# The cross-attention's mask written into the score banks by ScalarE and VectorE, with the order of the steps made anew

## The chip, the core and the metric

The kernel runs on one core of a Trainium2 chip. Its five engines run side by side and meet only at semaphores: TensorE (PE, with the load of its stationary operand shown apart as PEld), VectorE (DVE), ScalarE (ACT), GpSimd (POOL) and SyncE (SP), which issues most DMAs. The time is device time of one execution in microseconds (us). Three runs of the kernel before took 546.56, 554.24 and 556.15 us, a median of 554.24. The execution that the profile shows took 546.79 us.

## The reference, cut to what matters

One decoder layer on 16 sequences of 100 tokens, 256 wide: self-attention (16 heads of 16, rotary), cross-attention (16 heads of 64), and a feed-forward layer that sends every token to one of 14 experts, each with a residual and a layer norm. What the change touches is the mask of the cross-attention:

```python
scores = einsum('bhsk,bhtk->bhst', Q, K) / sqrt(64)
causal_ok = arange(Sk)[None, :] <= arange(Sq)[:, None]
pad_ok = arange(Sk)[None, :] < source_seq_len[:, None]
allowed = causal_ok[None, None] & pad_ok[:, None, None, :]
attn = softmax(where(allowed, scores, -1e6), axis=-1)
```

The mask depends on the sequence and not on the head. The context has 361 tokens, and the causal rule leaves the first 100 of them.

## The kernel before, in words

The attention part is one list of 1819 steps, `STEPS`, written out by hand or by a program. Every engine walks through the same list and does the steps that are its own; a step that needs another engine's result waits on a semaphore. So the list alone sets the order in which an engine takes its work, and an engine that waits holds back all that stands behind it in its own queue. After the list comes the experts' part, a loop over blocks of 128 rows.

Names of steps are `kind.side.sequence.half.unit`: side `s` is self-attention, `x` is cross-attention. A sequence has two halves of its heads, a half is a *pair* of units, a unit has 4 heads and a score tile of 100 x 400. The steps of one pair of the cross-attention:

- `scores` (TensorE): at L1298 two matmuls add the mask, `ident_neg` (the unit matrix times -1e6) times `mask_b`, one for each unit's bank, and open the banks; then at L1303 eight matmuls per unit's four heads and two units add the products of queries and keys. The two units use the upper and lower 64 rows of the array.
- `max` (VectorE, L1030), `exp` (ScalarE, L886, four instructions for the heads of a unit, each with its sum), `inv` (VectorE, L1035), `norm` (GpSimd, L798), `turn` (TensorE transposes, L1314), `copy_v` or `copy_a` (VectorE L1042 or ScalarE L895, out of the one bank for turned tiles), `pv` (TensorE, L1340), `o_hi` (ScalarE, L907) and `o_lo` (VectorE, L1050), then `wo`, `added`, `stats`, `rstd`, `ln` and the router.

Four banks hold scores: pairs take two of them in turn, so that the scores of pair p wait for the `exp` of pair p-2. The self-attention's `scores` fill all four. The projections `xT`, `qk`, `K`, `V`, `Q`, `wo` and others share two further banks. The weights `W_self`, `W_K`, `W_V`, `W_O` are split at the start into a high part (`w_hi`, ScalarE) and a low part (`w_lo_v` on VectorE at L961, `w_lo_p` on GpSimd at L773). `keys_v` (VectorE, L1024) or `keys_p` (GpSimd, L791) spreads the self-attention's keys.

Of the kernel before, what the change touches and what calls it, by code (L numbers as in the profile page):

```python
# [82 lines left out]
qkT_out.1 turn.s.0.0.0 mask.0 exp.s.0.1.1 K.0.1 keys_p.1 copy_v.s.0.0.0 rot_sum.2 w_hi.9 turn.s.0.0.1 inv.s.0.1
mask.1 norm.s.0.1.0 scores.s.1.0 copy_v.s.0.0.1 K_out.0.1 w_lo_v.9 norm.s.0.1.1 turn.s.0.1.0 K_out.0.0 pv.s.0.0
w_hi.10 max.s.1.0.0 qkT.2 qk.3 copy_v.s.0.1.0 qkT_out.2 w_lo_p.10 max.s.1.0.1 o_hi.s.0.0 exp.s.1.0.0 max.s.1.1.0
turn.s.0.1.1 o_lo.s.0.0 keys_v.2 K.0.2 copy_v.s.0.1.1 exp.s.1.0.1 max.s.1.1.1 qk_out.3 pv.s.0.1 exp.s.1.1.0
inv.s.1.0 v.2 rot.3 norm.s.1.0.0 o_hi.s.0.1 norm.s.1.0.1 exp.s.1.1.1 turn.s.1.0.0 o_lo.s.0.1 copy_v.s.1.0.0 v_out.2
turn.s.1.0.1 K_out.0.2 inv.s.1.1 out.0 rot_sum.3 norm.s.1.1.0 copy_a.s.1.0.1 scores.s.2.0 added.s.0 norm.s.1.1.1
stats.s.0 pv.s.1.0 turn.s.1.1.0 o_hi.s.1.0 max.s.2.0.0 rstd.s.0 qkT.3 copy_a.s.1.1.0 o_lo.s.1.0 V.0.0 max.s.2.0.1
qkT_out.3 ln.s.0 exp.s.2.0.0 keys_p.3 max.s.2.1.0 x_load.4 turn.s.1.1.1 V_out.0.0 yT.0 exp.s.2.0.1 bias.x.0  # L90
copy_v.s.1.1.1 K.0.3 yT_out_v.0 max.s.2.1.1 exp.s.2.1.0 inv.s.2.0 pv.s.1.1 norm.s.2.0.0 V.0.1 o_hi.s.1.1
norm.s.2.0.1 exp.s.2.1.1 o_lo.s.1.1 turn.s.2.0.0 V_out.0.1 K_out.0.3 copy_v.s.2.0.0 v.3 inv.s.2.1 norm.s.2.1.0
# [1596 lines left out]
```

How the kernel before makes its waits and increments, by code:

```python
    def __call__(self, sem, value):  # L310
        if self.seen.get(id(sem), 0) < value:
            self.seen[id(sem)] = value
            self.engine.wait_ge(sem, value)
# [417 lines left out]
                def check(b):  # L731
                    wait(lens_in, 16)
                    length = pool.value_load(len_row[0:1, b:b + 1])
                    with pool.If(length <= 0):
                        step, dma = fix_step, fix_dma[b]
                        pool.memset(fix_b[:, :], 0.0).then_inc(step, 1)
                        pool.wait_ge(step, 5 * b + 1)
                        pool.dma_start(fix_a[:, :], ctx[b, 0:P, :]).then_inc(dma, 16)
                        pool.dma_start(fix_b[0:TK - 2 * P, :], ctx[b, 2 * P:TK, :]).then_inc(dma, 16)
                        pool.wait_ge(dma, 32)
                        pool.tensor_tensor(fix_b[:, :], fix_a[:, :], fix_b[:, :], ALU.add).then_inc(step, 1)
                        pool.wait_ge(step, 5 * b + 2)
                        pool.dma_start(fix_a[:, :], ctx[b, P:2 * P, :]).then_inc(dma, 16)
                        pool.wait_ge(dma, 48)
                        pool.tensor_tensor(fix_b[:, :], fix_a[:, :], fix_b[:, :], ALU.add).then_inc(step, 1)
                        pool.wait_ge(step, 5 * b + 3)
                        pool.partition_all_reduce(fix_a[:, :], fix_b[:, :], P, bass.bass_isa.ReduceOp.add).then_inc(step, 1)
                        pool.wait_ge(step, 5 * b + 4)
# [844 lines left out]
    @block.vector  # L1593
# [13 lines left out]
        dve.wait_ge(tables_in, 32)
        dve.wait_ge(counts_ready, 1)
```

## Time and profile before

| | |
|---|---|
| time of the profiled execution | 546.79 us |
| its span, first to last instruction | 545.0 us |
| median of three runs | 554.24 us |
| TensorE busy | 486.0 us, 89% |
| VectorE busy | 361.8 us, 66% |
| ScalarE busy | 322.8 us, 59% |
| GpSimd busy | 216.1 us, 40% |
| mean granted clock of TensorE | 0.967 |

The page shows one execution. Section 1 gives each engine's busy time, section 2 cuts the span into 40 slices, and section 5 lists groups of instructions with their busy time, the mean length of one, and the idle time of the engine before them with what ended it. Busy shares are averages over stages: the attention's list takes the span up to about 456 us, the experts the rest from 465 us. A matmul's record is longer than its share of the engine, because matmuls overlap; the distance from one start to the next is what it takes.

### The profile page before, as it was taken

How to read it: one execution, taken by the hardware profiler on the slowest of the kernel's cores; microseconds unless marked ns; L12 is line 12 of the kernel's file. 1: busy time of each engine (PE TensorE's matmuls, PEld its weight loads, DVE VectorE, ACT ScalarE, POOL GpSimd, SP SyncE). 2: the span in 40 equal slices, each digit the busy share in tenths (PEclk: the TensorE clock that was granted, in tenths of full speed). 3: DMA queues.
4: the chain of work that ended last, by engine and by line, in shares of the span. 5: the costliest groups of instructions: out<-in, count | busy, mean ns of one | idle time of the engine just before them, and what ended most of it. 6: DMA issues, size and time to landing. Idle time of an engine off the chain costs nothing. (4 is left out here: it accounts for less than half of the span.)

```text
span 545.0 us, 13058 instructions
## 1 busy us (share of the span) xinstructions
PE 486.0 (89%) x4614; PEld 414.3 (76%) x4614; DVE 361.8 (66%) x1007; ACT 322.8 (59%) x1481; POOL 216.1 (40%) x309
## 2 busy tenths in 40 slices
PE   0667999999899999999999999999999871999992
PEld 0456787888689879888987888798798670899991
DVE  1788678688955875888588668856653833355563
ACT  2366678875747586867386876757573821433430
POOL 2246444443622553345245523543340511044343
PEclk9868999999999999999999999999999996899998
DMA  8960002910045008004500440180404522999300
GB/s 206 201 126 2 9 16 113 292 67 1 25 155 162 14 12 304 6 9 169 171 1 25 154 157 1 58 274 4 138 35 155 169 81 73 335 371 370 112 26 16
DMA packets 37577, 62.85 MB, mean 115 GB/s; under 512 B 9979, under 2 KB 30721, under 8 KB 36793
## 3 DMA queue, kind: packets, MB, share of 16 engines
q1 hardware_dynamic: 34668, 57.86, 32.8%
q0 software_dynamic: 1888, 3.30, 1.9%
q10 hardware_dynamic: 950, 0.80, 0.6%
q8 instruction: 39, 0.64, 0.5%
q14 instruction: 32, 0.26, 0.1%
HBM read 58.65 MB, written 29.77 MB: 162 GB/s over the span
## 5 line engine op out<-in xcount | busy, mean ns | idle before, releaser
L886 ACT ACTIVATE probs<-bank,neg_max 100x100 f32<-100x100 f32 x512 | 170.5, 379 | 17.9 <-DVE neg_max L1030 13.5
L798 POOL TENSOR_TENSOR probs<-probs,row_inv 100x400 f32<-100x400 f32 x128 | 112.1, 896 | 128.6 <-DVE row_inv L1035 128.6
L886 ACT ACTIVATION_READ_ACCUMULATOR probs<-bank,neg_max 100x1 f32 x512 | 123.3, 241 | 0.0
L1314 PE MATMUL bank<-ident,probs 100*100 100x100 f32 x512 | 67.3, 254 | 5.9 <-DVE probsT L1042 5.0
L1030 DVE TENSOR_REDUCE neg_max<-bank 100x4 f32<-100x400 f32 x128 | 68.2, 563 | 6.2 <-PE bank L1303 4.6
L1314 PEld LDWEIGHTS bank<-ident,probs 100*100 100x100 f32 x512 | 49.4, 128 | 18.3 <-issue 8.0
L1042 DVE COPY probsT<-bank 100x400 f32<-100x400 f32 x78 | 44.5, 571 | 22.7 <-PE bank L1314 21.8
L1169 PE MATMUL bank<-cT_h,W_K 128*128 128x200 f32 x256 | 50.2, 282 | 0.5 <-DVE vX L1060 0.3
L1234 PE MATMUL bank<-yT,W_Q 128*128 128x200 f32 x256 | 50.1, 339 | 0.4 <-ACT qX L932 0.4
L1169 PE MATMUL bank<-W_O,oX_h 128*100 128x256 f32 x256 | 46.7, 283 | 0.0
L1169 PE MATMUL bank<-W_self,xT_h 128*100 128x256 f32 (+1 forms) x128 | 36.8, 376 | 10.7 <-DVE cT_l L970 3.9
L895 ACT COPY probsT<-bank 100x400 f32<-100x400 f32 x50 | 25.2, 504 | 32.3 <-PE bank L1314 32.0
L1234 PEld LDWEIGHTS bank<-yT,W_Q 128*128 128x128 f32 x256 | 42.4, 190 | 2.1 <-ACT qX L932 0.6
L1547 ACT ACTIVATE hT<-bank,b1c 128x128 f32<-128x128 f32 x72 | 20.6, 369 | 38.6 <-PE bank L1497 38.6
L1169 PEld LDWEIGHTS bank<-cT_h,W_K 128*128 128x128 f32 x256 | 41.5, 192 | 1.6 <-issue 0.7
L1169 PE MATMUL bank<-W_V,cT_h 128*100 128x512 f32 x128 | 42.1, 409 | 0.6 <-DVE xs L1068 0.4
L802 POOL TENSOR_TENSOR rstd<-var_eps,half_power 100x1 f32<-100x1 f32 x32 | 17.8, 556 | 52.2 <-DVE var_eps L1081 50.4
L1497 PEld LDWEIGHTS bank<-xTs,w 128*128 128x128 f32 x288 | 35.7, 197 | 1.5 <-issue 0.7
L1497 PE MATMUL bank<-xTs,w 128*128 128x128 f32 x288 | 36.2, 281 | 0.3 <-ACT xTs L1537 0.3
L932 ACT ACTIVATE qX<-bank,q_bias_scaled 128x200 f32<-128x200 f32 x64 | 24.7, 452 | 19.3 <-PE bank L1234 19.3
L1169 PEld LDWEIGHTS bank<-W_O,oX_h 128*100 128x100 f32 x256 | 35.9, 165 | 0.4 <-issue 0.3
L1169 PE MATMUL bank<-W_O,oX_l 128*100 128x256 f32 x128 | 35.9, 281 | 0.0
(150 smaller groups left out, 1042.1 us busy)
## 6 DMA issues: line engine op xcount, KB each, us to landing
expert_rows<-c_empty SPq DMA_DIRECT2D x13, 1935.0 KB, 12.8
w<-in_L_ffn_w_dram SPq DMA_DIRECT2D x36, 512.0 KB, 7.3
cs<-in_ctx_dram SPq DMA_DIRECT2D x16, 100.0 KB
xs<-in_x_dram SPq DMA_DIRECT2D x13, 100.0 KB
...
```

The costliest lines, as they stand in the source:

```text
L798: probs_ready.mark(pool.tensor_tensor(v, v, r, ALU.mult), step)
L802: ln_rstd.mark(pool.tensor_tensor(rstd[:, s, :], var_eps[:, s, :], half_power[0:T, :], ALU.pow), step)
L886: i = act.activation(probs[:, k % SLOTS, w], sc_bank[p % 2 * 2 + u][0:T, w], ACT.Exp, bias=neg_max[:, k % SLOTS, h:h + 1], accum_out=row_s ...
L895: copied[kind].mark(act.copy(probsT[:, k % SLOTS, :], pt_bank[0:T, 0:UW]), step)
L932: i = act.activation(qX[:, g % 2, m, :], ps[:, h * GT:(h + 1) * GT], ACT.Identity, scale=DK ** -0.5, bias=q_bias_scaled[:, m:m + 1])
L1030: max_ready.mark(dve.tensor_reduce(neg_max[:, k % SLOTS, :], src, AX_X, ALU.max, negate=True), step)
L1042: copied[kind].mark(dve.tensor_copy(probsT[:, k % SLOTS, :], pt_bank[0:T, 0:UW]), step)
L1169: i = pe.matmul(ps, lefts[a][k], rights[b][k], start=(k == 0 and q == 0), stop=(k == n - 1 and q == 2))
L1234: i = pe.matmul(ps[:, h * GT:(h + 1) * GT], W_Q[:, c, m * P:(m + 1) * P], yT[:, c, :], start=(c == 0), stop=(c == KC - 1))
L1314: i = pe.transpose(pt_bank[0:T, h * T:(h + 1) * T], probs[:, k % SLOTS, h * T:(h + 1) * T], ident[0:T, 0:T])
L1497: i = pe.matmul(h_bank[n % 2][:, f * P:(f + 1) * P], w[:, c, f * P:(f + 1) * P], xTs[:, n % SLOTS_X, c, :], start=(c == 0), stop=(c == KC ...
L1547: i = act.activation(hT[:, n % SLOTS_X, f, :], h_bank[n % 2][:, f * P:(f + 1) * P], ACT.Gelu, bias=bias[f])
```

## The change

Nothing is left of the two mask matmuls. A new step, `masked_a` (ScalarE) or `masked_v` (VectorE), 16 of each, writes -1e6 times the mask into both banks of a pair, from `mask_b`, and the score products add to what stands there. The wait for the `exp` of pair p-2 and the wait for the mask move from TensorE to this step; TensorE waits for the step. `mask` (VectorE) now waits for the writes of the sequence two before, no longer for its scores. `ident_neg` is gone. In the self-attention's scores only the first matmul into a bank opens it. The order of the list is new throughout: 1851 steps, with 55 turned tiles copied by ScalarE (50 before) and 73 by VectorE (78 before), and 14 of the spreads of keys on GpSimd (6 before) and 2 on VectorE (10 before).

```diff
 STEPS = """
...
-check.4 qk.0 check.5 w_lo_v.2 check.6 qk_out.0 v.0 check.7 rot.0 xT.2 w_hi.3 bias.s.2 xT_hi.2 check.8 v_out.0 w_hi.4
...
+V_out.15.1 copy_a.x.14.0.1 masked_v.x.15.1 exp.x.15.0.0 pv.x.14.0 inv.x.14.1 norm.x.14.1.0 scores.x.15.1 o_hi.x.14.0
...
+MASKED = ("masked_a", "masked_v")
...
-    pairs = [pair for s in PLAN if s[0] == "scores" for pair in scored(s)]
+    pairs = [pair for s in PLAN if s[0] in MASKED or s[0] == "scores" and s[1] == "s" for pair in (scored(s) if s[1] == "s" else [s[1:]])]
+    scored_units = [pair + (u,) for s in PLAN if s[0] == "scores" for pair in scored(s) for u in range(2)]
...
+            def mask_banks(step):
...
+                p, b = pair_place[step[1:]], step[2]
+                one = mask_b[:, b % 2, :].unsqueeze(1).broadcast_to([T, UH, T])
+                return [(sc_bank[p % 2 * 2 + u][0:T, 0:UW].rearrange("p (h t) -> p h t", h=UH), one) for u in range(2)]
...
-                        act.activation(ident_neg[:, :], ident[0:T, 0:T], ACT.Copy, scale=NEG).then_inc(late_set, 1)
...
+                    elif kind == "masked_a":
+                        p = pair_place[step[1:]]
+                        if p >= 2:
+                            wait(*exp_ready.at(("exp",) + pairs[p - 2] + (1,)))
+                        wait(*mask_ready.at(("mask", step[2])))
+                        for out, one in mask_banks(step):
+                            i = act.activation(out, one, ACT.Copy, scale=NEG)
+                        bank_masked[kind].mark(i, step)
...
                         if n >= 2:
-                            wait(*scores_ready.at(("x", n - 2, 1, 1)))
+                            for c in range(2):
+                                wait(*masked(("x", n - 2, c)))
...
+                    elif kind == "masked_v":
+                        p = pair_place[step[1:]]
+                        if p >= 2:
+                            wait(*exp_ready.at(("exp",) + pairs[p - 2] + (1,)))
+                        wait(*mask_ready.at(("mask", step[2])))
+                        for out, one in mask_banks(step):
+                            i = dve.tensor_scalar(out, one, NEG, None, ALU.mult)
+                        bank_masked[kind].mark(i, step)
...
-                                                  kD[r, b % 2, half, :, :].rearrange("p h t -> p (h t)"), start=True, stop=True)
+                                                  kD[r, b % 2, half, :, :].rearrange("p h t -> p (h t)"), start=(half == 0), stop=(half == KC - 1), skip_group_check=True)
...
-                            if p >= 2:
-                                wait(*exp_ready.at(("exp",) + pairs[p - 2] + (1,)))
...
-                            wait(*mask_ready.at(("mask", b)))
-                            for u in range(2):
-                                pe.matmul(two[u][0:T, 0:UW].rearrange("p (h t) -> p h t", h=UH), ident_neg[:, :],
-                                          mask_b[:, b % 2, :].unsqueeze(1).broadcast_to([T, UH, T]), start=True, stop=False, skip_group_check=True)
+                            wait(*masked(step[1:]))
```

**Place 1, TensorE at the end of the list.** The rows are TensorE's from the last `Q` step of the kernel before (L1234) to the scores of pair x.14.1; `kX,qX` are score products, `cT,W_V` values, `ident,y` the turned output of sequence 13, `Wr,rT` the router. Before:

```order
L1234 MATMUL bank<-yT,W_Q 128x200 x4
L1169 MATMUL bank<-W_V,cT_h 100x512 x2
L1169 MATMUL bank<-W_V,cT_l 100x512
L1169 MATMUL bank<-W_V,cT_h 100x512 x2
L1169 MATMUL bank<-W_V,cT_l 100x512
L1298 MATMUL bank<-mask_b,ident_neg 100x400 x2
L1303 MATMUL bank<-kX,qX 100x100 x8
L1201 MATMUL bank<-ident,y 128x100 x2
L1298 MATMUL bank<-mask_b,ident_neg 100x400 x2
L1303 MATMUL bank<-kX,qX 100x100 x8
```

And of the change:

```order
L1235 MATMUL bank<-ident,y 128x100 x2
L1332 MATMUL bank<-kX,qX 100x100 x8
L1268 MATMUL bank<-yT,W_Q 128x200 x4
L1300 MATMUL bank<-Wr,rT 100x14 x2
L1203 MATMUL bank<-W_V,cT_h 100x512 x2
L1203 MATMUL bank<-W_V,cT_l 100x512
L1203 MATMUL bank<-W_V,cT_h 100x512 x2
L1203 MATMUL bank<-W_V,cT_l 100x512
L1203 MATMUL bank<-W_V,cT_h 100x512 x2
L1203 MATMUL bank<-W_V,cT_l 100x512
L1203 MATMUL bank<-W_V,cT_h 100x512 x2
L1203 MATMUL bank<-W_V,cT_l 100x512
```

The mask matmuls are gone, and the last `Q` step and the value step V.14.1 now stand behind the scores of x.14.0, in front of those of x.14.1.

**Place 2, VectorE at the start of the list.** The rows are VectorE's from the values of sequence 0 to the first `max`; `W_K` and `W_V` are low parts of weights, `kD` the spread keys that the first scores wait for. Before:

```order
L1016 TENSOR_TENSOR vS<-bank,qkv_bias 100x8x2x16
L961 TENSOR_TENSOR W_K<-kX,W_K 128x8x2x64
L970 TENSOR_TENSOR xT_l<-bank,xT_h 128x200
L1007 TENSOR_TENSOR rot<-rot,rot_b 100x512
L984 TENSOR_TENSOR qk<-bank,qkv_bias 100x512
L970 TENSOR_TENSOR cT_l<-bank,cT_h 128x2x100
L961 TENSOR_TENSOR W_V<-qX,W_V 128x8x2x64
L1024 TENSOR_TENSOR kD<-qkT,own 128x400
```

And of the change:

```order
L1042 TENSOR_TENSOR vS<-bank,qkv_bias 100x8x2x16
L995 TENSOR_TENSOR xT_l<-bank,xT_h 128x200
L1033 TENSOR_TENSOR rot<-rot,rot_b 100x512
L986 TENSOR_TENSOR W_K<-kX,W_K 128x8x2x64
L1010 TENSOR_TENSOR qk<-bank,qkv_bias 100x512
L1050 TENSOR_TENSOR kD<-qkT,own 128x400
L1027 TENSOR_TENSOR rot<-qk,rotary 100x32x8 x2
L1029 TENSOR_TENSOR rot_b<-qk,rotary 100x32x8 x2
L1056 TENSOR_REDUCE neg_max<-bank 100x4
```

The low part of `W_V` and one turned context (`cT_l`) moved from in front of `kD` to behind the first `max`; that of `W_K` stands behind `rot`.

**Place 3, VectorE in the steady part of the change.** The rows are around `masked_v.x.3.1`, with what each waits for; the same stretch returns every two sequences. `exp_ready` is the end of an `exp` on ScalarE.

```order
L1076 COPY probsT<-bank 100x400 [waits turned]
L1084 TENSOR_TENSOR oX_l<-bank,oX_h 128x400 [waits o_high]
L995 TENSOR_TENSOR xT_l<-bank,xT_h 128x200 [waits part_high]
L1094 TENSOR_TENSOR vX<-bank,v_bias 100x512 [waits projected]
L1003 SCALAR_TENSOR_TENSOR mask_b<-iota,len_f,later_sb 100x100 [waits bank_masked_a]
L1068 TENSOR_SCALAR bank<-mask_b 100x400 [waits mask_ready,exp_ready]
L1068 TENSOR_SCALAR bank<-mask_b 100x400
L1081 TENSOR_TENSOR oS_l<-bank,oS_h 128x100 [waits o_high]
L995 TENSOR_TENSOR cT_l<-bank,cT_h 128x2x100 [waits part_high]
L1061 RECIPROCAL row_inv<-row_sum 100x8
```

The two writes into the banks are new, and so is VectorE's wait for `exp_ready` in front of them; what other engines read from `oS_l` and `cT_l` stands behind it.

## Rows read from the trace of the kernel before

**Rows 1.** The page, section 1: busy us, share of the span, instructions.
```profile
PE 486.0 (89%) x4614; PEld 414.3 (76%) x4614; DVE 361.8 (66%) x1007; ACT 322.8 (59%) x1481; POOL 216.1 (40%) x309
```

**Rows 2.** Busy time by stage: stretch, length, busy of each engine, clock, DMA share, GB/s.
```profile
core 0: us, PE busy (x) PEld busy (x) DVE busy (x) ACT busy (x) POOL busy (x), PEclk, DMA share, GB/s
20.00:60.00 40.00, 29.87 (x239) 22.50 (x239) 35.65 (x68) 24.04 (x108) 19.98 (x30) 0.79 0.39 81
60.00:430.00 370.00, 364.92 (x3719) 310.18 (x3717) 265.35 (x745) 255.07 (x1227) 152.39 (x200) 1.00 0.27 93
430.00:465.00 35.00, 16.99 (x177) 13.93 (x176) 15.69 (x57) 11.80 (x48) 10.53 (x14) 0.85 0.38 132
```

**Rows 3.** TensorE from 203.77 us: start, length, line, operands, count; scores of a pair.
```profile
203.77 0.40 PE L1201 MATMUL bank<-ident,cs 100*128 100x100 f32 x2
204.00 0.50 PE L1298 MATMUL bank<-mask_b,ident_neg 100*100 100x400 bf16 x2
204.44 0.95 PE L1303 MATMUL bank<-kX,qX 64*100 64x100 f32 x16
```

**Rows 4.** The mask matmuls alone, by line: least, median, longest ns.
```profile
L1298 PE MATMUL bank<-mask_b,ident_neg x64: 330/332/372, 81.8 to 430.2; 100*100 100x400 bf16 x64
```

**Rows 5.** TensorE elsewhere: transposes before full-height products, and before score products of quarter height.
```profile
207.35 0.51 PE L1314 MATMUL bank<-ident,probs 100*100 100x100 f32 x4
207.63 0.34 PE L1169 MATMUL bank<-cT_h,W_K 128*128 128x200 f32 x1
...
298.20 0.51 PE L1314 MATMUL bank<-ident,probs 100*100 100x100 f32 x4
298.64 0.94 PE L1281 MATMUL bank<-kD,qkT 32*100 32x200 f32 x16
```

**Rows 6.** Rows that price the new writes and moved steps: least, median, longest ns.
```profile
L1042 DVE COPY probsT<-bank x78: 558/575/577, 39.8 to 436.3; 100x400 f32<-100x400 f32 x78
L895 ACT COPY probsT<-bank x50: 492/493/595, 52.8 to 442.1; 100x400 f32<-100x400 f32 x50
L1096 DVE TENSOR_SCALAR y<-xs,mean_var,rstd x16: 404/414/1023, 56.9 to 394.1; 100x256 f32<-100x256 f32 x16
```

**Rows 7.** Groups by line: busy us, mean ns of one, idle before and who ended it.
```profile
L886 ACT ACTIVATE probs<-bank,neg_max 100x100 f32<-100x100 f32 x512 | 170.5, 379 | 17.9 <-DVE neg_max L1030 13.5 <-PE bank L1314 4.0
L1024 DVE TENSOR_TENSOR kD<-qkT,own 128x400 f32<-128x400 f32 x10 | 6.7, 667 | 1.4 <-ACT qkT L875 1.4
```

**Rows 8.** VectorE at the start: weight split, first keys, rotary.
```profile
20.71 3.08 DVE L961 TENSOR_TENSOR W_K<-kX,W_K 128x1024 fp32r<-128x1024 f32 x1
...
26.00 1.23 DVE L961 TENSOR_TENSOR W_V<-qX,W_V 128x1024 fp32r<-128x1024 f32 x1 [0.47 <-ACT W_V L842]
27.18 0.57 DVE L1024 TENSOR_TENSOR kD<-qkT,own 128x400 f32<-128x400 f32 x1
```

**Rows 9.** GpSimd at the same time.
```profile
20.35 2.36 POOL L773 TENSOR_TENSOR W_K<-kX,W_K 128x1024 fp32r<-128x1024 f32 x1
```

**Rows 10.** TensorE at the start: first scores, and the stall after them.
```profile
27.81 1.66 PE L1281 MATMUL bank<-kD,qkT 32*100 32x200 f32 x16
...
33.88 1.18 PE L1169 MATMUL bank<-W_self,xT_h 128*100 128x512 f32 x2 [3.88 <-DVE cT_l L970]
```

**Rows 11.** TensorE at the end of the list: last Q step to a stall.
```profile
419.26 1.52 PE L1234 MATMUL bank<-yT,W_Q 128*128 128x200 f32 x8
420.47 0.78 PE L1169 MATMUL bank<-W_V,cT_h 128*100 128x512 f32 x2
...
422.00 0.50 PE L1298 MATMUL bank<-mask_b,ident_neg 100*100 100x400 bf16 x2
...
433.19 0.52 PE L1314 MATMUL bank<-ident,probs 100*100 100x100 f32 x4 [0.92 <-DVE probsT L1042]
```

**Rows 12.** The chain that ended last, by line, the page's section 4.
```profile
PE bank L1497 6%; PE bank L1508 5%; PE bank L1488 1%; DMA xin<-expert_rows 0%; DMA out_dram<-res,xin 0%; POOL rs L1581 0%; DVE summed L1642 0%; DVE st L1645 0%; DVE biased L1640 0%; DVE res L1655 0%; ACT xTs L1537 0%; SPq L1447 0%; DVE ve L1651 0%; DVE waiter L1648 0%; POOLq L1438 0%
```

More of the change, by code:

```diff
@@ L83 @@
[L83 to L92, printed above, removed]
@@ new lines @@
+masked_a.x.0.0 ln.s.2 o_lo.s.3.0 x_load.6 Q.0.2 qk_out.4 rot.4 v.4 Q_out.0.2 turn.s.3.1.0 v_out.4 Q.0.3
+copy_a.s.3.1.0 rot_sum.4 turn.s.3.1.1 Q_out.0.3 yT.2 copy_v.s.3.1.1 scores.x.0.0 bias.x.2 yT_out_a.2 masked_v.x.0.1
+pv.s.3.1 qkT.4 max.x.0.0.0 o_hi.s.3.1 cT.3 o_lo.s.3.1 qkT_out.4 scores.x.0.1 max.x.0.0.1 c_load.5 exp.x.0.0.0
+keys_p.4 out.3 mask.2 max.x.0.1.0 cT_hi.3 added.s.3 exp.x.0.0.1 cT_lo.3 xT.5 stats.s.3 xT.6 bias.s.5 xT_hi.5
+masked_v.x.1.0 xT_hi.6 bias.s.6 exp.x.0.1.0 rstd.s.3 xT_lo.5 scores.x.1.0 xT_lo.6 ln.s.3 K.1.0 inv.x.0.0 max.x.0.1.1
@@ new lines @@
+xT_lo.9 pv.s.7.0 V_out.5.1 cT.6 exp.x.4.1.1 qk.9 norm.s.7.1.0 mask.6 c_load.8 norm.s.7.1.1 cT_hi.6 masked_v.x.5.1
+o_hi.s.7.0 turn.s.7.1.0 scores.x.5.0 bias.s.9 copy_a.s.7.1.0 o_lo.s.7.0 cT_lo.6 turn.s.7.1.1 inv.x.4.1 qk_out.9
+norm.x.4.1.0 cT.7 copy_a.s.7.1.1 scores.x.5.1 max.x.5.0.0 c_load.9 cT_hi.7 norm.x.4.1.1 rot.9 exp.x.5.0.0 pv.s.7.1
+turn.x.4.1.0 v.9 o_hi.s.7.1 cT_lo.7 copy_a.x.4.1.0 o_lo.s.7.1 max.x.5.0.1 K.3.0 max.x.5.1.0 exp.x.5.0.1 v_out.9
+mask.7 turn.x.4.1.1 out.7 rot_sum.9 K_out.3.0 copy_v.x.4.1.1 exp.x.5.1.0 K.3.1 added.s.7 inv.x.5.0 max.x.5.1.1
@@ new lines @@
+pv.s.13.0 V_out.11.1 cT.12 exp.x.10.1.1 qk.15 norm.s.13.1.0 mask.12 c_load.14 norm.s.13.1.1 cT_hi.12 masked_v.x.11.1
+o_hi.s.13.0 turn.s.13.1.0 scores.x.11.0 bias.s.15 copy_a.s.13.1.0 o_lo.s.13.0 cT_lo.12 turn.s.13.1.1 inv.x.10.1
+qk_out.15 norm.x.10.1.0 cT.13 copy_a.s.13.1.1 scores.x.11.1 max.x.11.0.0 c_load.15 cT_hi.13 norm.x.10.1.1 rot.15
+exp.x.11.0.0 pv.s.13.1 turn.x.10.1.0 v.15 o_hi.s.13.1 cT_lo.13 copy_a.x.10.1.0 o_lo.s.13.1 max.x.11.0.1 K.6.0
+max.x.11.1.0 exp.x.11.0.1 v_out.15 mask.13 turn.x.10.1.1 out.13 rot_sum.15 K_out.6.0 copy_v.x.10.1.1 exp.x.11.1.0
@@ L249 @@
+turn.x.15.1.0 wo.14 copy_a.x.15.1.0 turn.x.15.1.1 added.x.14 pv.x.15.0 copy_a.x.15.1.1 stats.x.14 id.14 o_hi.x.15.0
+rstd.x.14 o_lo.x.15.0 ln.x.14 pv.x.15.1 rT.14 o_hi.x.15.1 rT_out.14 o_lo.x.15.1 logits.14 wo.15 logits_out.14
+added.x.15 stats.x.15 id.15 rstd.x.15 ln.x.15 rT.15 rT_out.15 logits.15 logits_out.15 top.7 gate.7 choose.7 count.7
+rank.7 place.7 scatter.14 scatter.15
 """
```

326 lines of the change are left out of this document (162 added, 164 removed).

## The prediction

> **What bounds the kernel now.** I read the busy shares first, then busy time by stage, then who waited for whom, then the timelines. The shares [rows 1] name TensorE, but an average over stages decides nothing. By stage [rows 2] the picture is clear: from 60 to 430 us TensorE is busy for 364.92 of 370 us, VectorE for 265.35 and ScalarE for 255.07. TensorE is the limit there, with 5.1 us of idle time in all, so what is taken off it counts almost in full, and what is laid on the two others costs nothing as long as it isn't late. From 20 to 60 us it is otherwise: VectorE is busy for 35.65 of 40 us, TensorE for 29.87, at a mean granted clock of 0.79. From 430 to 465 us nobody is full, and latency rules. The experts' part after that is a solid chain of TensorE's own [rows 12]; the change doesn't touch it.
>
> **The mask matmuls.** There are 64, two for each of 32 pairs [rows 4]. In the timeline the two start at 204.00 and the score products behind them at 204.44 [rows 3]: 0.44 us for a pair, 32 x 0.44 = 14.1 us in all. That is the most that can go. The two together last 0.50 and one alone 0.33 [rows 3, 4], so the second starts 0.17 behind the first, and two such distances are 0.34; the other 0.10 is a pause before the score products. It need not go with the masks, for the same pause shows where no mask stands: four transposes take 0.28 us in front of full-height products and 0.44 in front of products of a part of the array's height [rows 5]. So the least is 32 x 0.34 = 10.9 us. I take 0.35, near the lower end, since that pause has its own row: **-11.2 us**.
>
> The Trainium skill (TensorE: Matmul & The Clock Gate, Back-to-back issue gap) gives N/2.4 + 2.5 ns for a matmul of N columns at the full clock; for 400 columns that is an estimate of 0.169 us, 0.338 a pair, and 10.8 us in all. By the row of starts alone it would be 14.1. The trace agrees with the page for the matmuls themselves and holds 0.10 us beside them that the page's rule doesn't.
>
> **What the two others take over.** Each of the 64 writes is a 100 x 400 operation into a score bank. The trace has no write from SBUF into a bank; the nearest rows are copies of the same shape out of a bank, 492 ns on ScalarE and 575 on VectorE [rows 6]. So 32 writes are about 15.7 us on ScalarE and 18.4 on VectorE. Five copies of 0.49 move to ScalarE (+2.5) and off VectorE (5 x 0.575 = -2.9), and eight spreads of keys of 0.67 leave VectorE (-5.4) [rows 7]. In the steady part that gives ScalarE about 255 + 18 = 273 us and VectorE about 265 + 10 = 275, in a stretch shortened to some 359. Both stay at three quarters, so neither becomes the bound by its sum. Their cover is TensorE's own work, and if that cover were gone the writes would cost up to 34 us; it isn't, but single waits can appear.
>
> A write by VectorE could be longer than a copy. A `TENSOR_SCALAR` with one SBUF source took 404 ns at best and 1023 at worst [rows 6], and a `W_K` split on VectorE took 3.08 us while GpSimd ran its own of 2.36, against 1.23 for the same shape later [rows 8, 9]: VectorE and GpSimd hold each other up in some operations, not in the copy out of a bank (558 to 577 [rows 6]). If each of VectorE's writes were stretched by the 0.6 us between 404 and 1023, that would be 32 x 0.6 = 19 us on an engine with 84 us to spare; its price on the path is inside the next term.
>
> The Trainium skill (SBUF — State Buffer, Who interferes with whom) says that a VectorE instruction with at most one SBUF input and outside the two-port modes doesn't contend with GpSimd, and its VectorE page keeps an operand in PSUM out of those modes. By that the stretch is nought for the new write, and VectorE's term is the 18.4 us; by the row of `TENSOR_SCALAR` it would be up to 37.
>
> **New waits in the steady part.** What stands behind a `masked_v` on VectorE, when it waits for an `exp`, is `o_lo`, a turned context's low part or a copy for the next transpose, and TensorE waits for those. In the old order only 5.1 us of idle were left [rows 2]; with 0.35 us less of cover per pair and a write between `exp` and `scores`, I expect a little more. The steps have room: between the scores of a self-attention pair and their first transpose the new list has 5 us or more of TensorE's own steps in nearly all cases, each step at its length in the trace. None at all would be the best; the other end is 8 us, a quarter of a us for each of the 32 pairs. I take **+2 us**.
>
> **The start.** The first score products start at 27.81, right after the keys `kD` at 27.18 [rows 8, 10]. In front of the keys stood 1.23 us of `W_V`, a turned context, and 3.08 us of `W_K`. Now `W_V` and the context are behind the first `max`, and `rot` stands before `W_K`, so that the transposes of queries and keys can run under it: up to 3 us earlier. The stall of 3.88 us at 30 [rows 10] waits for a turned context behind four rotary operations on VectorE, and such a queue is still there. GpSimd's splits and its new spreads of keys can collide with the rotary operations instead. I take **-2 us**, between -4 (keys and stall both better) and +3 (one more collision of the size 3.08 - 1.23 = 1.9, and a stall at the lower clock).
>
> **The end of the list.** `Q` of 419.26 to 420.47 and V.14.1 up to 422.00 [rows 11] stood in front of the last four score steps: 2.7 us. They now stand between the first and the second, and are done while ScalarE does its first exponentials; afterwards TensorE had stood idle (0.92 us at 433.19 [rows 11], and 18 of 35 us [rows 2]). In return the second scores come later: before, 1.5 us behind the first, now behind one Q step and two V steps, about 5.5. ScalarE was already busy with two units of exponentials (8 x 0.33, from 170.5/512 [rows 7]) and a gate, so its third unit starts some 1.8 us later and its last some 0.9, with one mask write pair of 1.0 in its chain. That leaves -2.7 + 0.9: **-2 us**, between -4 and +1.
>
> **The sum.** -11.2 + 2 - 2 - 2 = -13.2, so the profiled execution's 546.8 us becomes 533.6. The three runs before were 546.56, 554.24 and 556.15: the profile lies at their fast end, 7.5 under their median. I can't tell which of the two levels the median of the changed kernel shows, so I put the number half-way between 533.6 and 541.0: **537 us**. Own range of this case: at best -14.1 + 0 - 4 - 4 = -22 (525 us), at worst -10.9 + 8 + 3 + 1 = +1 (548 us), 555 at the higher level.
>
> **Rivals.**
> - *The gain is given back.* TensorE's time is freed, but the list was dense, and it now stands where it once worked: scores wait for a mask write that waits for an `exp`, or a transpose for a copy that queued behind a write. For it: before, every pair's mask ran in an otherwise idle-free TensorE, and the new write lies on the way from `exp` to `scores`, with 1 us (2 x 0.49) where the matmuls had 0.44. Against it: most `masked` steps have two or more TensorE steps between them and their scores. Giving back 11.2 us takes a mean of 0.35 us a pair. Time 546.
> - *VectorE's wait holds back its queue: slower.* 16 `masked_v` steps sit on VectorE, and 9 of them stand one or two of its steps behind the last `exp` of the pair whose bank they take. If VectorE stands there until one unit's `exp` is through (4 x 0.33 = 1.3 us) and then writes for 1.0, everything queued behind is 2.3 us late; were TensorE to wait each time at all 16, that is 37 us, and at 12 of them 28: 546.8 - 11.2 + 28 = 563 us. It comes out slower than before from 0.7 us of TensorE's wait per `masked_v` on (11.2/16). Against it: VectorE is idle for 105 us of the 370 [rows 2].
> - *Better than the sum.* The new order also closes the 10 us of idle time at the start [rows 2] and keeps the full clock there. Time 522.
>
> **Chances.** The forecast 0.53, given back 0.27, the slower rival 0.14, better 0.06. A measurement of this kernel tells about 2%, 11 us, from no change. The forecast's gain of 13.2 us is just over that: 0.47 of its 0.53 is faster and 0.06 within. Of the rival of 546 0.26 is within and 0.01 faster, of the slower one 0.12 slower and 0.02 within, and the last is faster by 0.06. So faster 0.54, within 2% 0.34, slower 0.12. The range from 526 to 553 us leaves out the slower rival's 0.12 and the best case's 0.06.
>
> **What would show it.** No matmul with `mask_b` in the profile; TensorE's busy time about 11 to 16 us less, its instructions 64 fewer. The writes about 0.5 us each. The first score products before 27 us. Idle time of TensorE between 60 us and the end of the list's dense part between 5 and 13 us. The prediction is wrong if TensorE's waits for a mask write, for transposed tiles or for `o_lo` sum to more than 10 us, if the writes are well over 0.6 us, or if the dense part starts later than before.

## The result: slower by 1.5%, where 2% faster was forecast

| | before | after |
|---|---|---|
| median, us | 550.98 (546.56 to 556.15, 4 runs) | 557.24 (553.77 to 559.75, 4 runs) |
| ratio | | 1.0152, 95% interval 1.0097 to 1.0207 |
| profiled execution, us | 546.79 | 553.77 |
| its span, us, and mean clock | 545.0, 0.967 | 551.3, 0.955 |

The forecast was 537, its range 526 to 553; the time lies above both. It is slower by less than the 2% that the forecast called no change, but the interval leaves out 1. Each ratio in this document is formed from the fast runs of both kernels alone, so it is not the quotient of the medians, which take in every run.

### The profile page after: what moved, and what is told of

Its sections match the earlier page's. It is cut to its first block and busy times, and to the rows that moved or that the text cites. A ratio compares the mean times of both kernels' runs of the same rounds, so it can differ in the third digit from the quotient of the medians.

```text
span 551.3 us, 12991 instructions
## 1 busy us (share of the span) xinstructions
PE 483.6 (88%) x4550; PEld 413.5 (75%) x4550; DVE 373.0 (68%) x1025; ACT 337.7 (61%) x1518; POOL 218.8 (40%) x317
## 5 line engine op out<-in xcount | busy, mean ns | idle before, releaser
L816 POOL TENSOR_TENSOR probs<-probs,row_inv 100x400 f32<-100x400 f32 x128 | 109.6, 875 | 92.6 <-DVE row_inv L1061 91.8
L903 ACT ACTIVATION_READ_ACCUMULATOR probs<-bank,neg_max 100x1 f32 x512 | 120.9, 237 | 0.0
L820 POOL TENSOR_TENSOR rstd<-var_eps,half_power 100x1 f32<-100x1 f32 x32 | 17.7, 554 | 99.3 <-DVE var_eps L1115 99.3
L1203 PE MATMUL bank<-cT_h,W_K 128*128 128x200 f32 x256 | 52.7, 292 | 1.3 <-DVE qk L1010 0.9
L1076 DVE COPY probsT<-bank 100x400 f32<-100x400 f32 x73 | 41.6, 570 | 16.3 <-PE bank L1343 14.6
L1203 PEld LDWEIGHTS bank<-cT_h,W_K 128*128 128x128 f32 x256 | 43.1, 199 | 4.7 <-ACT kX L944 1.6
L920 ACT COPY probsT<-bank 100x400 f32<-100x400 f32 x55 | 27.4, 499 | 24.5 <-PE bank L1343 23.3
L1203 PE MATMUL bank<-cT_l,W_K 128*128 128x200 f32 x128 | 36.2, 283 | 0.0
```

Of the source, the lines that this page charges most:

```text
L816: probs_ready.mark(pool.tensor_tensor(v, v, r, ALU.mult), step)
L820: ln_rstd.mark(pool.tensor_tensor(rstd[:, s, :], var_eps[:, s, :], half_power[0:T, :], ALU.pow), step)
L903: i = act.activation(probs[:, k % SLOTS, w], sc_bank[p % 2 * 2 + u][0:T, w], ACT.Exp, bias=neg_max[:, k % SLOTS, h:h + 1], accum_out=row_s ...
L920: copied[kind].mark(act.copy(probsT[:, k % SLOTS, :], pt_bank[0:T, 0:UW]), step)
L1076: copied[kind].mark(dve.tensor_copy(probsT[:, k % SLOTS, :], pt_bank[0:T, 0:UW]), step)
L1203: i = pe.matmul(ps, lefts[a][k], rights[b][k], start=(k == 0 and q == 0), stop=(k == n - 1 and q == 2))
```

## The profile after

The page's busy shares, to be read beside [rows 1]:

```profile
PE 483.6 (88%) x4550; PEld 413.5 (75%) x4550; DVE 373.0 (68%) x1025; ACT 337.7 (61%) x1518; POOL 218.8 (40%) x317
```

TensorE has its 64 instructions fewer, but only 2.4 us less of busy time. Busy time by stage, beside [rows 2], with the same columns:

```profile
20.00:60.00 40.00, 31.32 (x245) 24.75 (x246) 34.88 (x66) 24.53 (x108) 18.19 (x30) 0.74 0.37 78
60.00:430.00 370.00, 355.07 (x3596) 302.60 (x3595) 271.87 (x750) 263.97 (x1235) 154.60 (x206) 0.99 0.27 93
430.00:465.00 35.00, 21.94 (x224) 17.79 (x222) 18.46 (x62) 15.41 (x75) 11.21 (x15) 0.90 0.34 119
```

From 60 to 430 us TensorE now idles for 14.9 us where it idled for 5.1, and it does 123 instructions fewer in the same 370 us. Of these, 63 are the mask matmuls; the other 60 are work that has moved out of this stretch, most of it to behind it. The two others stand at 272 and 264 us, near the 275 and 273 that the prediction gave them, so their sums are no bound.

The writes themselves, by line, shape by shape: least, median and longest ns, then whose idle time lay before them and who waited for them:

```profile
L1068 DVE TENSOR_SCALAR bank<-mask_b x32: 556/567/581, 82.0 to 437.3; 100x400 f32<-100x400 bf16 x32
its engine sat idle before it (us, times) until:
  ACT probs L903: 3.9, 5
who waited for it (us, times):
  PEld bank L1332: 0.4, 1
```
```profile
L912 ACT ACTIVATE bank<-mask_b x32: 498/546/631, 76.0 to 431.9; 100x400 f32<-100x400 bf16 x32
```

VectorE's last what its copies of that shape lasted (567 against 575 ns [rows 6]) and are not stretched by GpSimd, ScalarE's are a tenth longer than its copies (546 against 493). In front of its own VectorE stood idle for an exponential only 5 times, 3.9 us in all. TensorE hardly waits for a write. What it does wait for (line waited for, us in total, times, longest):

```profile
PE bank L1235 <- DMA xs<-in_x_dram: 6.9, 2, 4.5
...
PE bank L1343 <- DVE probsT L1076: 6.2, 8, 1.1
PE bank L1203 <- DVE vS L1042: 5.7, 2, 4.3
...
PE bank L1293 <- DVE so_far L1172: 3.9, 6, 1.8
```

`so_far` is the last result of the router's `choose`, which `rank` on TensorE needs. One of the places, 286 to 298 us; it comes back every two sequences, five times in all (turns 0 to 4 of the router, a turn being the routing of two sequences). TensorE (start, length, idle time before and its releaser in brackets):

```profile
290.42 0.40 PE L1203 MATMUL bank<-W_V,cT_l 128*100 128x512 f32 x1
291.22 0.19 PE L1293 MATMUL bank<-chosen,before_b 100*100 100x28 bf16 x1 [0.40 <-DVE so_far L1172]
291.26 0.20 PE L1294 MATMUL bank<-so_far,ones_b 100*100 100x28 bf16 x1
292.19 0.52 PE L1343 MATMUL bank<-ident,probs 100*100 100x100 f32 x4 [0.73 <-DVE probsT L1076]
...
294.09 1.16 PE L1203 MATMUL bank<-W_V,cT_h 128*100 128x512 f32 x2
```

VectorE and GpSimd at the same time:

```profile
287.37 0.56 DVE L1076 COPY probsT<-bank 100x400 f32<-100x400 f32 x1
287.85 2.31 DVE L1149 SCALAR_TENSOR_TENSOR candidate<-logits_all,top_logit,less 100x14 f32<-100x14 f32 x2
290.20 0.18 DVE L1153 TENSOR_REDUCE first_top<-candidate 100x2 f32<-100x28 f32 x1
...
290.91 0.17 DVE L1172 TENSOR_TENSOR so_far<-so_far,chosen 100x14 bf16<-100x14 bf16 x1
```
```profile
285.01 2.82 POOL L816 TENSOR_TENSOR probs<-probs,row_inv 100x400 f32<-100x400 f32 x3 [0.93 <-DVE row_inv L1061]
287.79 0.72 POOL L802 TENSOR_TENSOR y<-y,o_bias 100x256 f32<-100x256 f32 x1
288.47 0.85 POOL L816 TENSOR_TENSOR probs<-probs,row_inv 100x400 f32<-100x400 f32 x1
289.28 0.85 POOL L809 TENSOR_TENSOR kD<-qkT,own 128x400 f32<-128x400 f32 x1
```

The two `candidate` operations of 100x14 take 2.31 us, and they end (290.16) when GpSimd's unbroken run ends (290.13). Before, the same two took 0.38 to 0.40 us in six of eight turns and 1.06 at most: its `candidate`, with a median of 233 ns, mostly stands in a quiet place of the list. The Trainium skill (SBUF — State Buffer, Who interferes with whom) says that a VectorE instruction with two SBUF inputs contends with a GpSimd instruction that reads SBUF. The trace agrees, with 2.31 against 0.38 us.

`so_far` and the copy of the turned tile behind it are late, and TensorE stands for 0.40 and 0.73 us. At this place the clock then falls to the lower of its levels, 1.2 GHz, for most of a stretch of 4 us (mean 0.57 of 2.4 GHz from 293.5 to 297.5):

```profile
293.50:297.50 4.00, 4.00 (x30) 2.60 (x28) 2.29 (x7) 3.88 (x20) 2.40 (x3) 0.57 0.09 26
```

The V step in it took 2.79 us, the same step two sequences earlier and later 1.54 and 1.53. But the same waits stand in the three other quarters of the steady part, and there the clock stays up. The third quarter is the one with the fall; below it the fourth:

```profile
276.77:329.61 52.84, 51.27 (x515) 43.35 (x511) 40.42 (x110) 37.77 (x177) 22.70 (x30) 0.97 0.26 88
329.61:381.17 51.56, 49.91 (x513) 42.25 (x509) 39.46 (x109) 37.40 (x176) 21.86 (x29) 1.00 0.27 89
```

So the fall costs some 1.1 us, once. TensorE's busy time hardly fell for two reasons. Over the whole span the mean clock is lower, 0.955 against 0.967. And busy time counts pauses as work: in the three quarters at the full clock TensorE is busy for 50.0 us, where before had 50.4 for two sequences, although 1.4 to 1.5 us of its work is gone (worked out below). A matmul's record runs on past its share of the engine and covers the start of a pause: above, the last V matmul starts at 290.42 and the next instruction at 291.22. Such a matmul is otherwise followed after 0.23 us, so 0.57 us is lost, of which 0.40 counts as idle.

**A yardstick.** The list repeats itself every two sequences, so I measure the steady part from the first score product of pair x.4.0 to that of x.12.0, a quarter of it being two sequences. In after:

```profile
173.20 0.95 PE L1332 MATMUL bank<-kX,qX 64*100 64x100 f32 x16
...
381.17 0.95 PE L1332 MATMUL bank<-kX,qX 64*100 64x100 f32 x16
```

So 207.97/4 = 51.99 us; before (the first mask matmuls at 174.56 and 376.76) 50.55. Each is read from one execution, and a stretch at the lower clock is in it: without its one fall after has 51.71, the mean of the other three quarters. And by stretches, from the start of TensorE's step to the next named one:

| | to x.0.0 | to x.4.0 | to x.12.0 | to the last `rank` | sum |
|---|---|---|---|---|---|
| before | 81.8 | 92.8 | 202.2 | 78.4 | 455.1 |
| after | 81.5 | 91.7 | 208.0 | 80.5 | 461.7 |

Of the 6.5 us that the list became longer, the steady part holds 5.8 and the end 2.1.

## The experiments

Theory 1 at the outset: the move of the mask gains its 10 to 14 us, and the new list loses some 20. Theory 2: the writes cost it. In the table, before's median in the same rounds is in brackets. The last column is the yardstick; the mean granted clock in its stretch was 1.00, except 0.99 in after and new_order_all_on_scalar, 0.98 in old_order_all_on_scalar and late_choose, 0.97 in late_choose_keys_xload, 0.96 in old_order_mask_written and 0.95 in late_rank. So part of what the slowest lists lose is time at the lower clock.

| run | mask | median, us | ratio, 95% interval | two sequences, us |
|---|---|---|---|---|
| before | matmuls | | | 50.55 |
| after | writes | 557.2 (551.0) | 1.010 to 1.021 | 51.99 |
| old_order_mask_written | writes | 586.4 (554.1) | 1.048 to 1.077 | 55.47 |
| old_order_all_on_scalar | writes | 575.8 (554.1) | 1.026 to 1.057 | 53.85 |
| new_order_mask_on_pe | matmuls | 561.0 (554.1) | 1.002 to 1.030 | 52.30 |
| new_order_keys_on_vector | writes | 553.4 (554.1) | 1.002 to 1.013 | 51.37 |
| new_order_all_on_scalar | writes | 560.2 (556.1) | 1.000 to 1.015 | 52.14 |
| late_rank | writes | 582.2 (556.1) | 1.040 to 1.053 | 56.32 |
| late_choose | writes | 568.2 (556.1) | 1.015 to 1.028 | 53.77 |
| late_choose_keys_xload | writes | 569.8 (556.1) | 1.018 to 1.031 | 54.59 |
| choose_behind_copy | writes | 551.1 (552.7) | 0.999 to 1.008 | 50.86 |
| choose_behind_copy_mask_on_pe | matmuls | 554.0 (552.7) | 1.001 to 1.011 | 50.93 |
| no_mask_old_order | none | 546.8 (553.3) | 0.992 to 1.002 | 49.82 |
| no_mask_new_order | none | 555.1 (553.3) | 0.999 to 1.028 | 51.72 |
| no_mask_choose_behind_copy | none | 545.3 (553.3) | 0.986 to 0.997 | 50.02 |
| choose_behind_copy_writes_moved | writes | **543.5** (553.3) | 0.985 to 0.995 | 50.09 |
| only_write_to_scalar | writes | 551.6 (554.3) | 0.997 to 1.008 | 50.69 |
| only_low_part_early | writes | 551.6 (554.3) | 0.986 to 1.002 | 50.59 |
| writes_moved_mask_on_pe | matmuls | 561.2 (554.3) | 1.000 to 1.041 | 52.62 |

### The list and the mask, one at a time

```diff
 # old_order_mask_written, old_order_all_on_scalar: before's list, for each pair
 ... exp.s.9.0.1
+masked_v.x.6.0          # every other one masked_a; in the second kernel all
 ... scores.x.6.0
 # new_order_mask_on_pe: after's list and before's code
-masked_v.x.6.0
```

> The list of before, step for step, with nothing changed but the mask: the 32 writes are put in, each right behind the last exponential of the pair two places earlier, in turn on VectorE and on ScalarE (16 each), and the two mask matmuls of each pair are gone. Theory 1 (the writes gain what the matmuls cost, 32 x 0.43 = 13.8 us on TensorE, and it is the new list that loses about 20 us): 536 to 543 us beside 551 for before, ratio 0.975 to 0.985. Theory 2 (the writes themselves cost it: they load VectorE and ScalarE with 32 x 0.5 to 0.57 us and make TensorE wait behind the exponentials): 551 to 560 us, ratio 1.00 to 1.02.

> As the first of these runs, but all 32 writes on ScalarE, where the exponentials are that they wait for, so that no write waits for another engine. Theory 1: 536 to 543 us, and within 3 us of the run with both engines, since neither is the bound. Theory 2 by ScalarE's load (16 more writes of 0.5 us on an engine that is busy 61% of the time): slower than the run with both engines by 5 us or more. If the exponential that VectorE waits for held its queue, this one is faster than the mixed one by 3 us or more.

> The list of after without its 32 write steps, run by the code of before, so that TensorE adds the mask with two matmuls a pair again. Theory 1 (the new list is what loses): slower than after by the price of the mask matmuls, 568 to 573 us, ratio to before 1.03 to 1.04. Theory 2 (the writes lose, the list is harmless): 545 to 553 us, ratio 0.99 to 1.00.

Neither theory fits both lists. The new list does lose by itself (52.30 against 50.55 us), but the writes in it bring 0.3 (0.6 at the full clock), not 1.7; and in the old list they lose 3.3 to 4.9, more than theory 2 had. The median score step, counted from its own start, did become shorter by 0.43 us in all kernels with writes. In the old list only one place was tried for the writes, the earliest. In the old list with both engines, VectorE stood idle before its writes each time:

```profile
L1064 DVE TENSOR_SCALAR bank<-mask_b x32: 567/573/579, 70.2 to 458.2; 100x400 f32<-100x400 bf16 x32
its engine sat idle before it (us, times) until:
  ACT probs L899: 21.2, 16
```

With all writes on ScalarE nothing waits in front of them, and it is 10.6 us faster, but still slow. Its writes sit in unbroken runs of exponentials, ahead of the results that TensorE needs next. ScalarE, then TensorE:

```profile
185.19 0.93 ACT L908 ACTIVATE bank<-mask_b 100x400 f32<-100x400 bf16 x2
186.06 0.73 ACT L940 ACTIVATE kX<-bank,k_bias 128x200 f32<-128x200 f32 x2
...
187.95 0.52 ACT L916 COPY probsT<-bank 100x400 f32<-100x400 f32 x1
```
```profile
186.84 0.48 PE L1199 MATMUL bank<-W_self,xT_h 128*100 128x256 f32 x2 [1.10 <-ACT kX L940]
...
188.62 0.52 PE L1339 MATMUL bank<-ident,probs 100*100 100x100 f32 x4 [0.84 <-ACT probsT L916]
```

A pair of writes is 0.93 us of queue, and TensorE waits 1.10 and 0.84 us for what stands behind it. ScalarE's share of the time, 274 of 370 us in that stage, doesn't show this.

### What the new list loses

```diff
 # new_order_keys_on_vector (sequences 4, 6, ... 14)
-keys_p.10
+keys_v.10
 # new_order_all_on_scalar (all 16)
-masked_v.x.7.1
+masked_a.x.7.1
```

> After, with six of the key spreads (batch entries 4, 6, 8, 10, 12, 14) on VectorE again, where before has them; GpSimd keeps the others. If GpSimd's longer unbroken run of work is what stretches the two comparisons of the router on VectorE (0.38 to 2.31 us at 287.85) and makes the ranking late: about 1.5 to 2 us each time in 5 to 6 places, clock included, so 7 to 11 us faster than after, 546 to 550 us. If the stretch comes from the norms on GpSimd and not from the spread: no change from after (within 2 us), 555 to 559 us, or slower by the spreads' own time on VectorE.

> After, with VectorE's 16 mask writes given to ScalarE, in the same places of the list. If VectorE is the engine that the new order is short of (its copies come late behind choose and the spreads): 2 to 6 us faster than after. If ScalarE is as short, because its runs of exponentials leave no hole for a write of 0.5 us: slower than after, 560 to 566 us. If the engines' loads do not matter: within 2 us of after, 555 to 559.

The keys' spread on GpSimd is a part: 51.37 us for two sequences, 0.34 less than after at the full clock. The second `candidate` takes 886 ns instead of 1703 and again ends with GpSimd's run, so the norm in that run stretches it too. TensorE no longer waits behind V (0.57 us), but stands longer between `rank` and the turned tile behind it (1.2 us from start to start, 0.96 in after). The 4 us that the median gained are less than the 7 expected, and the two intervals overlap. The writes' engine makes no difference in this list (52.14). So VectorE is not short of time; it is late at single places. The next three kernels try the one around `choose` in the router's turns 0 to 4 (the diffs show turn 2).

```diff
 # late_rank: rank, place and both scatters later; late_choose: choose and count too
-scores.x.6.1 choose.2 count.2 bias.x.8
+scores.x.6.1 bias.x.8
 ... copy_v.x.6.0.1 yT_out_a.8 max.x.6.1.1
+choose.2 count.2
 ... cT_lo.8
+rank.2
 turn.s.9.1.1 inv.x.6.1
+place.2 scatter.4 scatter.5
 qk_out.11 norm.x.6.1.0
 # late_choose_keys_xload: with the six spreads on VectorE as well, and
-xT.5 stats.s.3 xT.6
+xT.5 stats.s.3
 ... scores.x.1.1
+xT.6
```

> After, with rank, place and the scatters of five of the eight turns (0 to 4) some six TensorE steps later; choose stays where it is. If TensorE's 0.85 us at each rank (and the wait of the turn behind it) is a wait for so_far alone: 0.9 to 1.5 us less in each of five places, with a clock drop saved, 551 to 554 us beside 557 for after. If it is the copies queued behind choose on VectorE that TensorE really waits for: the wait moves to the turned tile behind V.n.0 and less than 2 us in all is gained, 555 to 558 us.

> As the run before it, and choose and count too stand later, behind the copy of the turned tile and the second maximum on VectorE instead of ahead of them. If VectorE's queue behind choose is what costs: 1.5 to 2.3 us less in each of five places than after, 545 to 550 us, and faster than the run with the late rank alone by 3 us or more. If only the rank's own wait counted: the same as that run within 2 us. If the new order loses elsewhere: 555 us or more.

> The late choose, with the six key spreads on VectorE and xT.6 behind the score step x.1.1, so that TensorE does not wait for the load of that sequence at 86 us (2.4 us, and 1.6 us at the lower clock behind it). If the three stalls are apart: 2 to 4 us less than late_choose, 541 to 547 us, below before's 551 to 554. If they share one cause or hide each other: the same as late_choose.

All three missed, by my own edit: the two scatters had come to stand ahead of the norms of x.6.1 on GpSimd, as late_rank's timelines show (GpSimd, then TensorE):

```profile
261.35 1.08 POOL L830 DMA_INDIRECT expert_rows<-y,place_i  x1 [5.46 <-issue]
262.74 1.03 POOL L830 DMA_INDIRECT expert_rows<-y,place_i  x1 [0.30 <-issue]
263.79 1.66 POOL L812 TENSOR_TENSOR probs<-probs,row_inv 100x400 f32<-100x400 f32 x2
```
```profile
264.70 0.57 PE L1339 MATMUL bank<-ident,probs 100*100 100x100 f32 x2 [2.33 <-POOL probs L812]
```

The scatters wait for `place_i` and take 2.4 us, five times. The wait of 2.33 us and the lower clock (0.95 against 0.99 of 56 us, an estimate of 2.3 us) make up the 4.3 us that late_rank loses to after in two sequences. That late_choose is 14 us faster than late_rank, in spite of the same scatters, is the sign that `choose` ahead of the copies does cost. With xT.6 moved, the wait for its load became one for a mask write: the score step x.1.0 stood 1.65 us for VectorE. Two stalls stood one behind the other there, and the third edit bought nothing.

```diff
 # choose_behind_copy: choose and count as in late_choose, and
 qk.11 ... cT_hi.8
+cT_lo.8
 masked_v.x.7.1
+rank.2
 turn.s.9.1.0 scores.x.7.0 bias.s.11
+place.2
 ... norm.x.6.1.1
+scatter.4 scatter.5
 # choose_behind_copy_mask_on_pe: without the masked steps, before's code
```

> After, with only the router's steps of turns 0 to 4 in other places: choose and count behind the copy of the turned tile on VectorE, rank behind qk three steps later than there, place right behind it, and the two scatters on GpSimd behind the norms that the next turn needs (in the run late_choose they stood ahead of them, which cost 2.4 us in each of five places). Theory: of after's 52.0 us for two sequences, the 0.86 at rank and about 0.9 at V go and nothing takes their place: 49.9 to 50.5 us for two sequences, and with five such places 8 to 10 us less than after in all, 546 to 550 us, at or just below before. Rival: TensorE's wait moves on to another late result of VectorE: 51.5 us or more for two sequences, 555 us or more.

> The same list without its 32 write steps, the mask added by matmuls. In after's list the writes took 0.43 us from each score step and gave back most of it elsewhere (52.0 us against 52.3 for two sequences). If that was since TensorE waited for VectorE at choose anyway, so that work saved ahead of it only made the wait longer, then with the wait gone the whole of it shows: this one is slower than choose_behind_copy by 11 to 14 us, 1.6 to 1.8 us for two sequences. If the writes themselves cost (as they did in the old list, 3 to 5 us for two sequences): slower by less than 6 us, or not slower.

The first was right in direction and short in size: 50.86 us, 1.13 less than after (0.85 at the full clock) and outside its 49.9 to 50.5; the median fell by 6, not 8 to 10. Nor need all of it be the router's: the edit also moved `cT_lo` of the turn's first sequence ahead of a mask write, which the expectation doesn't name, and no run has it alone. `candidate` is back at its length:

```profile
L1145 DVE SCALAR_TENSOR_TENSOR candidate<-logits_all,top_logit,less x16: 221/226/235, 134.7 to 455.8; 100x14 f32<-100x14 f32 x16
```

In the second the theory missed: with matmuls 50.93 us, so the writes still brought 0.07, and 2.9 us by the medians.

### The same lists without any mask

```diff
-                            for u in range(2):
-                                pe.matmul(two[u]..., ident_neg[:, :], mask_b..., start=True, stop=False, ...)
...
-                                                  start=False, stop=(h == UH - 1), skip_group_check=True)
+                                                  start=True, stop=True, skip_group_check=True)
```

> Leaves the cross-attention's mask out (its output is not the reference's): before, its list unchanged, without the mask matmuls and without writes. If the saving is real and the writes take it back: the whole 0.43 us per score step shows, 11 to 14 us less than before, 537 to 542 us, 48.8 to 49.3 us for two sequences against 50.55. If the saving is worth little by itself since TensorE would wait for VectorE and ScalarE: 5 us or less, 547 us or more.

> Leaves the mask out: the list of after without writes and without mask matmuls. If the writes take the saving back: 50.6 us for two sequences against 52.3 with the matmuls and 52.0 with the writes, 10 us or more less than after, about 547. If TensorE waits for the steps around choose anyway: 51.7 to 52.0 us, within 3 us of after.

> Leaves the mask out: the list of choose_behind_copy without writes and without mask matmuls. If the writes take the saving back: 49.2 to 49.5 us for two sequences against 50.9 with either form of the mask, 538 to 543 us. If the saving is worth little by itself: 50.5 us or more, 548 us or more.

First, how much work is gone. TensorE in the old list without a mask, and below it the row that follows in before on those of [rows 3]:

```profile
203.45 0.40 PE L1197 MATMUL bank<-ident,cs 100*128 100x100 f32 x2
203.78 0.95 PE L1296 MATMUL bank<-kX,qX 64*100 64x100 f32 x16
204.66 0.55 PE L1307 MATMUL bank<-ident,probs 100*100 100x100 f32 x4
```
```profile
205.32 0.55 PE L1314 MATMUL bank<-ident,probs 100*100 100x100 f32 x4
```

From the turned context `ident,cs` to the step behind the scores it takes 1.21 us without the mask and 1.55 with it (203.77 to 205.32). So 0.34 us is gone, and not 0.43: the pause of 0.1 us in front of the score products stays, and now stands in the step ahead of them (0.33 us instead of 0.23). In the new list 24 of the 32 pairs save 0.34 so, and seven, whose step in front is itself a product on a part of the array, 0.47. With 0.34 for the last, which a wait hides, that is 11.8 us in all and 1.4 to 1.5 us for two sequences. It brought this:

| list | matmuls | none | writes | gained without a mask | taken back by the writes |
|---|---|---|---|---|---|
| old | 50.55 | 49.82 | 53.85 to 55.47 | 0.73 | 4.0 to 5.7 |
| after's | 52.30 | 51.72 | 51.99 | 0.58 | 0.27 |
| choose_behind_copy | 50.93 | 50.02 | 50.86 | 0.91 | 0.84 |

So two to three fifths of TensorE's saving show, since the next step then waits for VectorE or ScalarE; the saving is worth less than its length in every list. The writes take it back in two of them. In after's list the 0.27 is no more than the one fall of the clock, which is 0.28 of the 51.99; in the old list part is the lower clock as well. In the old list even the gain is lost again at the end: TensorE reaches pair x.14.0 at 417.6 us without a mask and at 422.0 with it, and the last `rank` at 455.2 and 455.1. The ratio for that kernel, 0.992 to 1.002, does not leave out 1, though the medians are 6.5 us apart.

### A list that carries the writes

```diff
-cT_lo.8 masked_v.x.7.1 rank.2
+cT_lo.8 masked_a.x.7.1 rank.2
 ... scatter.4 scatter.5
+cT_lo.9
 rot.11 ...
```

> choose_behind_copy with two more moves in turns 0 to 4: the second write of the odd sequence goes from VectorE to ScalarE, right behind the exponentials that it waits for, and cT_lo of the second sequence stands ahead of the rotary products on VectorE instead of behind them. If what TensorE waits 0.7 us for at v.7, v.9 and so on is cT_lo behind the write and place: 50.1 to 50.3 us for two sequences, 3 to 4 us less than choose_behind_copy, 546 to 548 us, and below before by 1%. If ScalarE's own results come late in turn: no change within 2 us.

It is faster than both kernels: 543.5 us, 0.990 of before (0.985 to 0.995), and 50.09 us for two sequences, the pace of choose_behind_copy without any mask (50.02). VectorE in choose_behind_copy, and below it in this one, at the same steps:

```profile
242.58 1.04 DVE L1064 TENSOR_SCALAR bank<-mask_b 100x400 f32<-100x400 bf16 x2
...
245.60 1.45 DVE L1023 TENSOR_TENSOR rot<-qk,rotary 100x256 f32<-100x256 f32 x2
246.98 0.74 DVE L1025 TENSOR_TENSOR rot_b<-qk,rotary 100x256 f32<-100x256 f32 x2
247.65 0.35 DVE L991 TENSOR_TENSOR cT_l<-bank,cT_h 128x200 fp32r<-128x200 f32 x1
```
```profile
242.15 0.37 DVE L991 TENSOR_TENSOR cT_l<-bank,cT_h 128x200 fp32r<-128x200 f32 x1 [0.39 <-ACT cT_h L874]
242.43 0.75 DVE L1023 TENSOR_TENSOR rot<-qk,rotary 100x256 f32<-100x256 f32 x2
243.10 0.75 DVE L1025 TENSOR_TENSOR rot_b<-qk,rotary 100x256 f32<-100x256 f32 x2
```

In the first, K.4.0 stood 0.54 us for `cT_l`, and the first two rotary products took 1.45 us beside GpSimd's norms (244.72 to 246.39), in the second 0.75, since `cT_l` goes first and the norms are nearly through (240.80 to 242.47). The expectation had 3 to 4 us of the 7.5. The steady part holds 3.1 of them; 2.6 more are gained from x.0.0 to x.4.0, which holds turn 0 and where choose_behind_copy had a stretch at the lower clock and this kernel had none (mean 0.98 and 1.00).

The last three kernels have one of the two moves each, and both moves without the masked steps, run by before's code.

> choose_behind_copy with only the five second writes of the odd sequences (5 of 32) given to ScalarE; cT_lo stays behind the rotary products. If it is the write of 1.05 us in VectorE's queue that makes cT_lo late: 50.1 to 50.4 us for two sequences, about all of the gain, 543 to 547 us. If it is cT_lo's own place: 50.8, about 551.

> choose_behind_copy with only cT_lo of the second sequence moved ahead of the rotary products in turns 0 to 4; the write stays on VectorE. If the write alone is to blame: 50.6 or more for two sequences, 549 to 551 us. If the place of cT_lo is enough: 50.1 to 50.4 us, 543 to 547, and both single moves give about the same.

> The list of choose_behind_copy_writes_moved without its write steps, the mask added by matmuls. If TensorE sets the pace here: 50.8 to 50.95 us for two sequences as in choose_behind_copy_mask_on_pe (cT_lo's move can't help it), 552 to 555 us, so that the writes are worth 0.8 us for two sequences and 8 to 10 us in all. If cT_lo's move also helps the matmul form: below 50.5 us and less than 5 us between the two.

Neither move does it alone: 50.69 and 50.59 us for two sequences, medians at 551.6. And the mask matmuls in this list cost 52.62 us and 561.2: here the writes are worth 10.1 us in the steady part and 17.7 by the medians (of only four runs, 556.5 to 567.1), and here the expectation missed. That is 2.5 us for two sequences, more than the matmuls' 1.5. The rest is a wait that choose_behind_copy_mask_on_pe doesn't have, in all four quarters:

```profile
252.82 0.49 PE L1165 MATMUL bank<-W_self,oS_h 128*100 128x256 f32 x2 [0.58 <-DVE vS L1012]
```

`out`, the projection of the self-attention's result, starts 0.83 us behind the last transpose instead of 0.03, since VectorE copies `vS` late; and a K step behind it waits 0.31 us for ScalarE's `kX`. So this pair of kernels measures the list with its matmuls as much as the matmuls.

## Why the prediction was wrong

- **The mask matmuls, -11.2 us.** The price of the work was right: 0.34 us in most pairs and 11.8 in all, with the pause of 0.1 us left standing as the prediction had it. What failed is the sentence in front of it, that what is taken off TensorE "counts almost in full", read from 5.1 us of idle time. The kernels without a mask show 0.6 to 0.9 of 1.4 to 1.5 us. A full engine says that nobody makes it wait at its present pace, not by how much they are ahead.
- **The new waits, +2 us, 0 to 8.** The step that failed most. Only waits around the writes had been costed, and in after's list they are indeed small: the writes gave 7.1 us by the last `rank` (468.7 with matmuls, 461.7 with writes), 3.7 by the medians. The order was taken as free, and it costs 13.6 us with the mask still on TensorE (468.7 against 455.1). Of the 1.75 us for two sequences that it loses, 0.86 stand behind `rank`, where TensorE waits for the turned tile (0.96 us from start to start, 0.10 before). The largest place found, `choose` beside GpSimd's run, was in neither the sum nor the rivals, though the prediction had just read from [rows 8, 9] that the two engines hold each other up; the moved key spreads were counted only as time that leaves VectorE.
- **The start, -2 us.** First scores at 28.8 instead of 27.8 us, so that sign was wrong; by x.0.0 the two kernels are level, -0.3. From 86 us on TensorE waited 2.4 us for the load of sequence 6, which the new list wants earlier.
- **The end, -2 us.** From x.12.0 on it takes 80.5 against 78.4 us: +2.1, outside its -4 to +1. No run changes this part alone, and why it is longer stays open.
- **Together** -0.3 - 1.1 + 5.8 + 2.1 = +6.5 us, for -13.2.
- **The rivals.** "The gain is given back" (546) was nearest in kind and stopped at zero. "VectorE's wait holds back its queue" describes what happens in the old list: 16 waits and 21.2 us of idle VectorE, 1.3 us each as it said, though the time, 586, is far above its 563. In after it is 3.9 us in 5 times; the new order, on whatever ground it was chosen, has room at these places and has none at others. "Better" had no part.
- **The signs.** The matmuls gone and writes of 0.5 to 0.6 us came true. TensorE's busy time fell by 2.4 and not by 11 to 16, since it counts part of the pauses and the time at the lower clock; its idle time in the stage is 14.9, over the 13 named. TensorE's waits for a mask write and for turned tiles are 9.0 us by the trace's own count, under the 10 named; `rank`'s 3.9 for `so_far` it had not named.
